# Graph-attention layer on one core: the opening and the passage to the edge loop redone

## The reference

```python
hn = jnp.maximum((x - mean(x)) / jnp.sqrt(var(x) + 1e-5), 0.0)   # each row of 256
h = hn @ W.T
src, dst = h @ a1, h @ a2
e = jax.nn.leaky_relu(src[:, None] + dst[None, :], negative_slope=0.2)
e = jnp.where(adj == 0, -9e15, e)
out = x + jax.nn.softmax(e, axis=1) @ h
```

## Time and profile before

| | |
|---|---|
| median of 3 runs | 403.71 us (402.9 to 403.84) |
| the profiled execution's own time | 403.5 us |
| its span, first to last instruction | 401.9 us |
| PE, DVE, ACT, POOL busy | 96%, 92%, 50%, 6% of the span |
| opening, until the first `project` | 0 to 12.6 us |
| projection loop | 12.6 to 44.3 us |
| passage, until the first `product` | 44.3 to 50.0 us |
| edge loop | 50.0 to 397.5 us |

### The profile page before, as it was taken

One profiled execution on the slowest core, in us unless ns is written; L12 is line 12 of the kernel. 1 busy time (PEld: TensorE's weight loads), 2 busy tenths in 40 slices (PEclk: granted clock), 3 DMA queues, 4 the chain that ended last, 5 costly groups with the idle time before them and its releaser, 6 DMA issues.

```text
span 401.9 us, 9634 instructions
## 1 busy us (share of the span) xinstructions
...
## 2 busy tenths in 40 slices
...
GB/s 220 367 95 2 2 205 274 234 186 196 195 189 189 169 237 235 222 223 223 213 218 210 207 174 226 221 215 223 221 221 180 170 227 215 219 225 221 179 0 106
DMA packets 26261, 77.90 MB, mean 194 GB/s; under 512 B 3296, under 2 KB 8960, under 8 KB 26112
## 3 DMA queue, kind: packets, MB, share of 16 engines
...
...
## 4 chain that ended last, share of the span: by engine, by line
PE 62%; DVE 21%; issue 8%; DMA 5%; DVEq 2%; ACT 1%; SPq 1%; ACTq 0%
PE ps L821 58%; DVE p_lo L624 8%; DVE p_sb L617 3%; DVE v_sb L586 3%; DMA adj_sb<-adj_t 2%; DMA x_sb<-x 1%; DVE stats L490 1%; DMA c_flat<-c_turned 1%; PE ps L783 1%; DVEq L586 1%; DVE rows_sb L684 1%; PE ps L768 1%; PE ps L779 1%; PE ps L780 1%; DVE hnt_lo L506 1%
## 5 line engine op out<-in xcount | busy, mean ns | idle before, releaser
L821 PE MATMUL ps<-v_sb,p_hi 128*128 (+2 forms) x2048 | 253.1, 272 | 2.5 <-ACT p_hi L431 1.3
L419 ACT ACTIVATE p_hi<-p_sb,p_scale 128x1024 f16<-128x1024 f32 x127 | 145.7, 1149 | 171.0 <-DVE p_sb L617 147.7
L821 PEld LDWEIGHTS ps<-v_sb,p_hi 128*128 128x128 f16 x2048 | 197.8, 97 | 31.9 <-ACT rows_sb L443 2.4
L624 DVE SCALAR_TENSOR_TENSOR p_lo<-p_sb,p_scale,p_hi 128x1024 f16<-128x1024 f32 x128 | 163.2, 1276 | 7.6 <-ACT p_hi L419 7.6
L617 DVE SCALAR_TENSOR_TENSOR p_sb<-c_row,g_col,adj_sb 128x1024 f32<-128x1024 uint32 (+1 forms) x127 | 161.8, 1276 | 1.8 <-DMA adj_sb<-adj_t 1.8
L821 PE MATMUL ps<-v_sb,p_lo 128*128 (+1 forms) x1024 | 141.6, 273 | 3.0 <-DVE p_lo L624 3.0
L821 PEld LDWEIGHTS ps<-v_sb,p_lo 128*128 128x128 f16 x1024 | 97.2, 97 | 21.7 <-DVE p_lo L624 9.5
L338 POOL DMA_DIRECT2D out<-rows_sb x24 | 13.2, 550 | 275.7 <-DVE rows_sb L641 274.3
L490 DVE BATCH_NORM_STATS2 stats<-x_sb 128x6 f32<-128x256 f32 x32 | 12.6, 402 | 7.7 <-DMA x_sb<-x 7.7
L353 ACT ACTIVATE h_sb<-ps 128x258 f32<-128x258 f32 x32 | 12.2, 380 | 3.2 <-PE ps L783 2.2
L768 PE MATMUL ps<-ident,hn_sb 128*128 128x128 f32 x64 | 12.3, 279 | 1.4 <-DVE hn_sb L513 0.8
...
## 6 DMA issues: line engine op xcount, KB each, us to landing
adj_sb<-adj_t SPq DMA_DIRECT2D x128, 512.0 KB, 4.7
...
w_nat<-w SPq DMA_DIRECT2D x1, 256.0 KB, 2.8
w_f<-w_t SPq DMA_DIRECT2D x1, 256.0 KB, 3.7
a_sb<-a SPq DMA_DIRECT2D x2, 1.0 KB, 3.0
```

Of the source, the lines that this page charges most:

```text
L419: nc.scalar.activation(p_hi[:, u % R, :], p_sb[:, u % R, :], ACT.Copy, scale=p_scale[:, bass.ds(t, 1)])\
L624: nc.vector.scalar_tensor_tensor(out=p_lo[:, u % R, :], in0=p_sb[:, u % R, :], scalar=p_scale[:, bass.ds(t, 1)], in1=p_hi[:, u % R, :], op ...
L821: return nc.tensor.matmul(ps[:, k, 0:width], part[:, u % R, k * P:(k + 1) * P], v_sb[:, bass.ds(t, 1), v, 0:width], start=start, stop=stop ...
```

## The change

- The vectors: `a1` and `a2` are loaded as four rows of 128 (`a_rows`), turned by one PE transpose and copied by DVE. They and `w_f` are issued on ACT's queue; `x` stands second on SP's, its first four tiles in two pieces.
- The norms: ACT squares W from `w_nat` and the vectors themselves, no longer `wa`; the scaling takes one root with a small bias and one reciprocal.
- The orders: ACT's and DVE's instructions of the projection loop are written out one by one. Statistics come in batches of 2 for the first eight tiles. Turned tiles use three PSUM banks, not four. PE puts `turn(t + 2)` behind `project(t)` for the first eight tiles, and half of `spread_s` behind the eighth.
- POOL normalises the odd tiles from 5 on (14, before 8), ACT 1, 3 and the even ones from 4 on (16, before 15), DVE 0 and 2 (before 9 tiles). POOL also makes `w1_hi` and `w1_lo` and the small scale factors, which DVE made.
- The chain for D: DVE keeps a running minimum already scaled, PE transposes it spread over 128 columns, so that one reduction leaves the number on all partitions (`exp_bias`). ACT takes the exponential for `c_row` straight from PSUM with it as bias; one exponential gives `g_col` and `p_scale` together. The exponential's table is loaded ahead, and DVE keeps `h` of tile 30.
- `c_flat`: DVE transposes `c_col` in blocks of 32 x 32 in the fourth step of the first round; SP stores it with four DMAs, each with rows of 32 floats.
- The values of tiles 0 to 7 (`v_sb`) are made by DVE, both parts, inside the projection loop; the first round of the edge loop has no `values_lo`.
- Matmuls without a reader: 5, 1, 1, 1; none in the passage.

```diff
-    BUSY_START, BUSY_SPLIT, BUSY_C = 6, 8, 5
+    BUSY_START, BUSY_SUMS, BUSY_SPLIT, BUSY_FIRST = 5, 1, 1, 1
-    BY_VECTOR = [0, 2] + list(range(4, T, 4))
-    BY_SCALAR = [1] + sorted([*range(5, T, 4), *range(6, T, 4)])
-    BY_GPSIMD = list(range(3, T, 4))
+    X_CHUNKS = [(0, 2), (2, 4)] + [(a, a + XB) for a in range(XB, T, XB)]
+    BATCHES = [(a, a + 2) for a in range(0, 2 * XB, 2)] + [(a, a + XB) for a in range(2 * XB, T, XB)]
+    BY_VECTOR = [0, 2]
+    BY_SCALAR = [1, 3] + list(range(4, T, 2))
+    BY_GPSIMD = list(range(5, T, 2))
+    EARLY_V = U
...
-        banks_t = (4, 5, 1, 0)
+        banks_t = (4, 5, 1)
...
-            for n, a in enumerate((a1, a2)):
-                sp.dma_start(a_sb[:, :, n], a.rearrange("(c p) -> p c", p=P),
-                             allow_slow_non_contiguous=True).then_inc(w_nat_loaded, 16)
-            sp.dma_start(w_f[:, :, 0:F], w_tv).then_inc(w_t_loaded, 16)
...
-            sp.wait_ge(c_turned_kept, 1)
-            sp.dma_start(c_flat, c_turned[:]).then_inc(c_flat_stored, 16)
-            sp.wait_ge(c_flat_stored, 16)
+            sp.wait_ge(c_blocks_ready, 1)
+            for b in range(P // T):
+                sp.dma_start(c_flat[:, b * T:(b + 1) * T], c_blocks[b * T:(b + 1) * T, :]).then_inc(c_flat_stored, 16)
+            sp.wait_ge(c_flat_stored, 16 * (P // T))
...
+                if t == BY_GPSIMD[0]:
+                    pool.wait_ge(w_hi_ready, 2)
+                    nc.gpsimd.tensor_copy(w1_hi[:], w_hi[:, :, F:F + 1].to_broadcast([P, KC, P])).then_inc(w1_ready, 1)
...
+                    for n, factor in enumerate((-0.8, 0.8, 0.2, -0.2, -0.8 * H_DOWN)):
+                        nc.gpsimd.tensor_scalar(exp_scale[:, n:n + 1], wa_norm[:], factor / H_UP, None, ALU.mult)\
+                            .then_inc(scales_ready, 1)
...
+            for n, a in enumerate((a1, a2)):
+                act.dma_start(a_rows[n * KC:(n + 1) * KC, :], a.rearrange("(c p) -> c p", p=P)).then_inc(a_loaded, 16)
+            act.dma_start(w_f[:, :, 0:F], w_tv).then_inc(w_t_loaded, 16)
...
+            split_hn_hi(31)
+            keep_h(29)
+            nc.scalar.activation(table_ready[:], eps_sb[:], ACT.Exp)
             act.wait_ge(d_part_ready, 1)
             keep_h(T - 1)
...
+                nc.scalar.activation(c_row[:, k0 * P:k1 * P], ps[:, bank, column:column + (k1 - k0) * P], ACT.Exp,
+                                     bias=exp_bias[:, 0:1], scale=exp_scale[:, 4:5]).then_inc(c_exp_ready, 1)
...
+            exp_c(0)
+            act.wait_ge(gp_args_ready, 1)
+            nc.scalar.activation(gp[:], gp_args[:], ACT.Exp).then_inc(gp_ready, 1)
+            exp_c(1)
+            exp_c(2)
...
+            def value_hi(t):
+                dve.wait_ge(h_kept, t + 1)
+                nc.vector.tensor_copy(v_sb[:, t, 0, 0:F], h_sb[:, t, 0:F]).then_inc(v_hi_early, 1)
+
+            def value_lo(t):
+                dve.wait_ge(v_hi_early, t + 1)
+                nc.vector.tensor_tensor(v_sb[:, t, 1, 0:F], h_sb[:, t, 0:F], v_sb[:, t, 0, 0:F], ALU.subtract)\
+                    .then_inc(v_lo_ready, 1)
...
+            nc.vector.tensor_reduce(exp_bias[:], ps[:, bank_d, 0:P], AX.X, ALU.min).then_inc(c_bias_ready, 1)
...
-                        values_lo(q * U + u, q * U + (u + 1))
+                        if not first:
+                            values_lo(q * U + u, q * U + (u + 1 - EARLY_V))
                         split_lo(u - 1, q * U + (u - 1), q * U)
+                    if first and u == 3:
+                        dve.wait_ge(c_col_ready, 1)
+                        nc.vector.transpose(c_blocks[:], c_col[:]).then_inc(c_blocks_ready, 1)
...
             for t in range(T):
-                if t + 2 < T:
+                if RB <= t < T - 2:
                     turn(t + 2)
                 project(t)
+                if t < RB:
+                    turn(t + 2)
+                if t == RB - 1:
+                    pe.wait_ge(w1_ready, 2)
+                    spread_s(0, 0)
+                    spread_s(0, 1)
+
+            spread_s(1, 0)
             pe.wait_ge(d_part_ready, 1)
-            nc.tensor.transpose(ps[0:1, bank_d, 0:P], d_part[:], ident[:]).then_inc(d_turned, 1)
...
+            nc.tensor.transpose(ps[:, bank_d, 0:P], d_lowest[:, 3:4].to_broadcast([P, P]), ident[:]).then_inc(d_turned, 1)
             spread_s(1, 1)
-            keep_busy(banks_t[1], BUSY_C)
```

More of the change, by code:

```diff
@@ new lines, in _ @@
+            nc.scalar.activation(w_hi[:, :, F:FW], wa_in_psum, ACT.Copy, scale=wa_scale[:, 0:1]).then_inc(w_hi_ready, 1)
+            normalise(1)
+            split_hn_hi(0)
+            split_hn_hi(1)
+            normalise(3)
+            std_of(2)
+            split_hn_hi(2)
+            keep_h(0)
+            normalise(4)
+            split_hn_hi(3)
+            keep_h(1)
+            std_of(3)
+            split_hn_hi(4)
+            keep_h(2)
+            normalise(6)
+            split_hn_hi(5)
@@ new lines, in _ @@
+            keep_h(3)
+            split_hn_hi(6)
+            keep_h(4)
+            std_of(4)
+            split_hn_hi(7)
+            normalise(8)
+            keep_h(5)
+            keep_h(6)
+            split_hn_hi(8)
+            normalise(10)
+            std_of(5)
+            keep_h(7)
+            normalise(12)
+            split_hn_hi(9)
+            split_hn_hi(10)
+            normalise(14)
+            keep_h(8)
+            std_of(6)
+            split_hn_hi(11)
+            keep_h(9)
@@ new lines, in _ @@
+            keep_h(17)
+            normalise(22)
+            split_hn_hi(20)
+            keep_h(18)
+            split_hn_hi(21)
+            keep_h(19)
+            normalise(24)
+            keep_h(20)
+            split_hn_hi(22)
+            split_hn_hi(23)
+            normalise(26)
+            keep_h(21)
+            split_hn_hi(24)
+            keep_h(22)
+            split_hn_hi(25)
+            std_of(9)
+            keep_h(23)
+            split_hn_hi(26)
+            normalise(28)
@@ new lines, in _ @@
+            stats_of(21)
+            split_hn_lo(12)
+            stats_of(22)
+            gather(21)
+            stats_of(23)
+            gather(22)
+            split_hn_lo(13)
+            stats_of(24)
+            gather(23)
+            split_hn_lo(14)
+            stats_of(25)
+            split_hn_lo(15)
+            stats_of(26)
+            rstd_of(7)
+            value_hi(0)
+            split_hn_lo(16)
+            split_hn_lo(17)
+            gather(24)
+            gather(25)
+            stats_of(27)
@@ new lines, in _ @@
+            gather(26)
+            gather(27)
+            value_hi(1)
+            split_hn_lo(18)
+            rstd_of(8)
+            stats_of(28)
+            value_hi(2)
+            split_hn_lo(19)
+            split_hn_lo(20)
+            value_lo(0)
+            split_hn_lo(21)
+            stats_of(29)
+            stats_of(30)
+            value_hi(3)
+            value_hi(4)
+            gather(28)
+            value_hi(5)
+            split_hn_lo(22)
+            gather(29)
+            stats_of(31)
@@ new lines, in _ @@
+            gather(30)
+            split_hn_lo(23)
+            split_hn_lo(24)
+            gather(31)
+            value_lo(1)
+            rstd_of(9)
+            split_hn_lo(25)
+            value_lo(2)
+            value_lo(3)
+            value_hi(6)
+            split_hn_lo(26)
+            split_hn_lo(27)
+            value_lo(4)
+            split_hn_lo(28)
+            value_lo(5)
+            split_hn_lo(29)
+            value_hi(7)
+            split_hn_lo(30)
+            value_lo(6)
```

431 lines of the change are left out of this document (250 added, 181 removed).

## The result

The changed kernel takes 399.55 us (median of six runs, 398.01 to 400.77) against 403.67 (402.9 to 403.84) for the kernel before, run beside it: a ratio of 0.9902, 95% interval 0.9882 to 0.9922. That is 1% faster. The forecast was 397.2 with a range of 394.5 to 401.0, so time and direction came out inside it, 2.35 us above the point. Its profiled execution took 398.96, 4.54 less than the 403.5 of before.

A forecast was written before the change was run, and what follows sets the result against it. PE was taken to bound the edge loop, so only its entry into steady state could move. Opening and projection loop 4.0 us plus passage 2.3 gave 6.3 off: 403.5 - 6.3 = 397.2 us, range 394.5 to 401.0.

The forecast's parts named there:

- The opening: Start to first project matmul: at 8.65 us, 3.9 us earlier than 12.58; bounds 7.9 and 9.8.
- norms 6.5, inverse 6.7: Opening: norms of the weights and vectors ready at 6.5 us, their inverse at 6.7.
- PE's floor is 29.7: Projection loop: PE needs 28.4 us for 32 tiles plus 1.3 for spread_s; 2.0 idle time was added.
- rival (d): PE's clock falls around the passage, slowing matmuls over most of one tile: costs about 2, 399.2 us; chance 0.08.
- rival (b): Projection loop: POOL's small factor instructions cost 1.34 each and hold tile 11's normalise; 400.7 us, chance 0.07.
- rival (a): Projection loop: DVE's value instructions wait for POOL, some 4 us come through; 401.2 us, chance 0.13.
- The passage: Last project to edge loop: first product 3.4 us behind it, tile 3's p_sb ends 9.85 behind, 2.9 less than before.
- What becomes of it: Wait for tile 8's edges: c_flat store and reload 0.6 us later, leaving the passage 2.3 us gain, bounds 0.1 and 2.9.
- what comes behind the store is bandwidth and can't shrink: Loads ahead of tile 8: DMA was full at 358 GB/s, so the time behind the c_flat store stays.
- saved for nothing: First round of the edge loop: dropping values_lo of tiles 4 to 7 gains nothing, as they end in tile 8's wait.
- (c): Passage: store and reload of c_flat becomes dearer, 2.8 us instead of 0.6; 399.4 us, chance 0.10.
- (e): Projection loop: POOL becomes the bound, at 2.5 us a tile, slower than before; 407.5 us, chance 0.04.

The follow-up runs named there:

- e5: Changed kernel with DVE's inverse of the norms and what hangs on it ahead of the statistics of x's second piece; 398.49 us.
- e3: Changed kernel with readerless matmuls added both in the opening (6 and 3 for 5 and 1) and in the passage (8); 400.35 us.
- e4: Changed kernel with POOL's small scale factors put behind its last tile; 398.71 us.
- e7: Changed kernel with the edits of e1, e4, e5 and e6 together; 394.87 us, ratio 0.9787 to the kernel before.
- e8: Changed kernel without early values: those of tiles 0 to 7 are made in the edge loop as before; 399.42 us.
- e10: Changed kernel with e6's order of loads and e8's lack of early values; 399.12 us.
- e6: Changed kernel with the 1.5 MB load of c_row put behind the edge loads of the second round on SP's queue; 395.81 us.
- e1: Changed kernel with 8 readerless matmuls in the passage, behind the last spread matmul; 401.19 us.
- e12: Changed kernel with DVE's block transpose of c_col in step 1 instead of 3 of the first round, for earlier stores; 399.86 us.
- e9: Kernel before with one edit, the 1.5 MB load of c_row behind the second round's edge loads; 401.51 us.

## Why the prediction came out as it did

**The opening: right in its kind, one term off by 0.96 us.** DVE began on x at 4.68 (forecast 5.0), and the norms came as forecast (6.48 for 6.5). The step that failed is "norms 6.5, inverse 6.7": it followed what the inverse needs and not what it stands behind on DVE. The second piece of x landed at 6.52 in this trace (6.3 to 7.9 over the changed kernel and its variants) and held it to 7.30. e5 shows the cause, and with it out of the way S is 8.64 for a forecast of 8.65. The changed kernel's runs spread over 2.8 us, for 0.9 before; this transfer is not the reason, as e5 takes it off the path and still spreads over 2.6. The reason is open.

**The projection loop: wrong by 1.7 us.** The forecast kept H - S at 31.7 and it became 33.4; H came at 43.01, a hair outside the 37.6 to 43 that the prediction had set as its own sign of being wrong (the sum behind the 43, 9.8 + 29.7 + 3.4, is 42.9). The step "PE's floor is 29.7" took full rate from the first matmul. Before, the rate doubled at 11.8, `project` began at 12.58 and its matmuls stood at 0.11 us from the first; now it starts at 9.61 and runs through matmuls at double distance until 13.3. This is rival (d) in a place where I had not put it. Its sentence "all rows have 1.00" read the clock column of 0 to 12.57 us, which has a record only from 11.76 on; the row of 16 matmuls in 3.76 us, shown above, gave the slow rate away before the change. By the slope of e3 it makes 3.7 x 0.37 = 1.4 us. POOL's factors ahead of tile 11 make 0.7 (e4; 0.5 in e7): rival (b)'s place, at 0.22 an instruction and not its 1.34. Without both, 33.4 would be 31.3, 0.4 under the forecast, so the floor and the idle time of the forecast were sized about right for a PE at full rate.

**The values beside POOL: rival (a) did not come.** `value_hi` took 280 ns on average (254 to 330) and `value_lo` 445 (385 to 618), with POOL busy for 60% of the loop. The four us of rival (a) would have needed waits of half a POOL tile, 0.67 us; the longest `value_lo`, 618, is 0.2 above the 385 to 420 of those with no POOL work beside them. What is there lies on POOL's side. Without the value instructions its tiles take 1221 on average (e8, from 8 to 42 us), with them 1268:

```profile
L341 POOL TENSOR_SCALAR hn_sb<-x_sb,moments,rstd 128x256 f32<-128x256 f32 x14 | 17.0, 1221 | 17.9 <-DVE shift L616 17.9
```

The difference is four tiles, those with value instructions beside them, at 1278, 1325, 1350 and 1554; it is 0.6 us in all, on an engine with idle time. The Trainium skill, SBUF — State Buffer, section Who interferes with whom, says that such pairs exclude each other for their whole length. The trace agrees that they delay each other, by up to 0.33 us for a POOL tile, and not that a DVE instruction waits for the end of POOL's 1.2 us: one `value_lo` of 417 ns lies wholly inside the tile of 1554. A loop without the 16 instructions (e8 and e10 against after and e6) was about 0.5 us shorter. The range for `value_hi`, 0.09 to 0.34, held; 0.34 was a little dear.

**The passage: right at its front.** First product H + 3.68 for 3.4, T = H + 9.91 for 9.85.

**What becomes of it: direction right, two terms off the other way.** The `c_row` load came 0.9 later by T, as against 0.6. But "what comes behind the store is bandwidth and can't shrink" did not hold in this execution: 9.56 us became 8.25. So R came at H + 26.55 for 27.5 and paid back 0.95 of what the loop had lost. That these errors were opposite is luck, and why the total is only 1.76 us off in the profiled execution: in e1 and e3 the same stretch took 9.6 and 9.7, and R came at H + 27.8 and 28.0. The cause of the 1.3 stays open (above).

**What bounds the kernel: partly wrong.** The prediction read "PE is busy for 275.95 of 277.5 us" as PE's loop. The point that enters the sum, that the end follows from the restart, holds: own time less R is the same within 0.02 us. But the row starts at 120 us and is for the most part the three groups without `values_lo`. In group 0 DVE sets the pace: e6 shows PE at 139 instructions in 15 us where the loop gives it 135, in e1 and e12 PE restarts at half clock and the end does not move, and what e6 and e9 win is DVE's wait for tile 8 and not PE's. From this view the edges' wait is not only 1.76 us of PE: it destroys whatever lead DVE had built. So the prediction wrote off the `values_lo` of tiles 4 to 7 as "saved for nothing" with the right result (e8 is 0.97 us behind after at T and 1.07 at R, both counted from H) and did not see that one changed position of a load would turn them into 3.3 us.

Of the other rivals, (c) did not come (landings of 2.1 to 2.8 us), nor (e). Rival (d) came a second time in the passage, at 1.2 GHz for about three microseconds (47.5 to 50.9), and cost nothing, as T = H + 9.91 with and without it shows.
